# A causal attention and expert kernel: values one chunk later and split, maxima, projections and output products at other chunks

## The reference

```
l2 = max(norm(xn), 1e-12);  normed = xn / l2 * sqrt(128) * gamma
q, k, v = split(normed @ w_qkv)            # 16 heads of 64
sim = (q / 8) @ k^T, causal;  attn = softmax(sim)
attention = concat_heads(attn @ v) @ w_out
router_w = the two best of 8 experts, softmax of their logits
experts = layer_norm(xn + sum_e router_w[e] * (relu(xn @ W1[e]^T + b1[e]) @ W2[e]^T + b2[e]))
```

## Time and profile before

| | |
|---|---|
| median of 3 runs | 1487.04 us (1483.02 to 1488.01) |
| the profiled execution | 1485.95 us |
| its span | 1484.2 us |
| TensorE busy | 94% |
| VectorE busy | 74% |
| ScalarE busy | 71% |
| POOL busy | 64% |

### The profile page before, as it was taken

How to read it: one execution, slowest core, us unless ns; L and a number is a source line. 1 busy time by engine, 2 the same in 40 slices (tenths; PEclk the granted TensorE clock), 3 DMA queues, 4 the chain that set the end, 5 groups by cost and what they waited for, 6 DMA issues and landing times.

```text
span 1484.2 us, 27052 instructions
## 1 busy us (share of the span) xinstructions
PE 1396.8 (94%) x8618; PEld 1069.1 (72%) x8618; DVE 1104.8 (74%) x1928; ACT 1058.7 (71%) x2589; POOL 947.7 (64%) x933
## 2 busy tenths in 40 slices
PE   3689999599999999999999999999999999999996
PEld 3679999367777777777777777777777777777774
DVE  6645555458876987698769876987688768876985
ACT  2556666377777777777777777777777777777774
POOL 1774000168667866786678667866786678667775
PEclk9689999799999999999999999999999999999998
DMA  9122221122212221221122212221212121212112
GB/s 328 63 89 64 68 58 51 39 49 53 49 44 59 53 51 43 59 55 47 44 62 53 50 41 63 51 49 43 63 51 49 44 62 50 49 44 62 50 44 75
DMA packets 77226, 89.89 MB, mean 61 GB/s; under 512 B 17656, under 2 KB 54816, under 8 KB 77088
## 3 DMA queue, kind: packets, MB, share of 16 engines
q1 hardware_dynamic: 59168, 69.90, 18.6%
q10 hardware_dynamic: 13824, 9.86, 2.1%
q0 software_dynamic: 4096, 8.40, 2.0%
HBM read 37.25 MB, written 16.78 MB: 36 GB/s over the span
## 4 chain that ended last, share of the span: by engine, by line
PE 58%; DVE 11%; POOL 6%; issue 4%; ACT 2%; DMA 1%; SPq 0%; POOLq 0%
PE max_ps L1271 9%; PE head_ps L1313 7%; PE head_ps L1315 7%; PE head_ps L1317 7%; PE score_ps L1297 7%; PE score_ps L1296 6%; DVE row_max L1123 4%; POOL p_lo L1037 4%; PE misc_ps L1247 3%; PE misc_ps L1327 3%; POOL two_y L1030 2%; PE max_ps L1274 2%; PE misc_ps L1241 2%; PE score_ps L1299 2%; PE misc_ps L1243 2%
## 5 line engine op out<-in xcount | busy, mean ns | idle before, releaser
L1037 POOL TENSOR_TENSOR p_lo<-probs,p_hi 128x512 fp32r<-128x512 f32 (+3 forms) x768 | 805.5, 1068 | 322.5 <-ACT p_hi L1075 317.5
L1075 ACT ACTIVATE probs<-score_ps 128x512 f32<-128x512 f32 (+3 forms) x768 | 376.5, 490 | 211.8 <-PE score_ps L1299 116.7
L1123 DVE TENSOR_REDUCE row_max<-max_ps 128x1 f32<-128x128 f32 (+7 forms) x512 | 385.9, 754 | 174.0 <-PE max_ps L1274 169.0
L1075 ACT ACTIVATE p_hi<-score_ps 128x512 fp32r<-128x512 f32 (+3 forms) x768 | 375.3, 489 | 0.0
L1313 PE MATMUL head_ps<-p_hi,v_hi 128*65 128x512 f32 (+3 forms) x768 | 289.3, 377 | 2.2 <-POOL p_lo L1037 1.3
L1271 PE MATMUL max_ps<-k_a,q_a 128*128 128x384 f32 (+5 forms) x768 | 259.8, 393 | 26.2 <-DVE row_max L1123 20.8
L1296 PE MATMUL score_ps<-q_a,k_a 128*128 128x512 f32 (+3 forms) x768 | 266.5, 347 | 2.5 <-DMA q_b<-shift 2.5
L1297 PE MATMUL score_ps<-q_b,k_b 65*128 65x512 f32 (+3 forms) x768 | 267.7, 349 | 0.0
L1317 PE MATMUL head_ps<-p_lo,v_hi 128*65 128x512 f32 (+3 forms) x768 | 258.8, 337 | 0.0
L1315 PE MATMUL head_ps<-p_hi,v_lo 128*64 128x512 f32 (+3 forms) x768 | 258.7, 337 | 0.0
L1296 PEld LDWEIGHTS score_ps<-q_a,k_a 128*128 128x128 f32 x768 | 144.9, 189 | 45.2 <-issue 3.4
(11 more groups left out here) (162 smaller groups left out, 2193.6 us busy)
## 6 DMA issues: line engine op xcount, KB each, us to landing
k_a<-k_a SPq DMA_DIRECT2D x64, 256.0 KB, 4.0
q_b<-q_a SPq DMA_DIRECT2D x64, 256.0 KB, 4.8
scale<-inv_rows SPq DMA_DIRECT2D x128, 128.0 KB, 2.9
sorted_x<-zeros SPq DMA_DIRECT2D x13, 384.0 KB, 16.4
sorted_y<-result ACTq DMA_DIRECT2D x78, 64.0 KB, 1.7
w_raw<-sorted_x SPq DMA_DIRECT2D x25, 192.0 KB, 2.5
acc<-in_L_attn_x_dram SPq DMA_DIRECT2D x4, 512.0 KB, 6.9
w_raw<-in_L_ffn_W_dram ACTq DMA_DIRECT2D x1, 2048.0 KB, 23.2
```

What stands on the lines that cost most here:

```text
L1037: pool.tensor_tensor(p_lo[:, slot, 0:w], probs[:, n_chunk(g, c) % PROBS, 0:w], p_hi[:, slot, 0:w].bitcast(F32), ALU.subtract).then_inc(p_s ...
L1075: ins = act.activation(p[:, n_chunk(g, c) % ring, 0:width], score_ps[n_chunk(g, c) % 2][:, 0:width], ACT.Exp, scale=SCALE)
L1123: dve.tensor_reduce(row_max[:, g % 2, t:t + 1], src, axes, ALU.max).then_inc(max_taken, 1)
```

## The change

The values run five chunks behind their scores (LAG 5), and every step of the chain is due one chunk later. The values are split: `pv` makes the two products with p_hi, waits only for ScalarE, and stands right behind the score; `pv_low` makes the product with p_lo, waits for POOL, and stands behind the maximum. ScalarE's raw copy follows `pv_low`. Part 6 of the maxima moves from chunk 10 to 9, the last projection from chunk 10 to 8, the first y from chunk 11 to 10 and the second from chunk 10 to 8 of the odd head. One combine step of each head moves from chunk 4 to 7. In the experts' part the second register load is dropped.

```diff
--- before.py
+++ after.py
@@ -695,8 +695,7 @@
                             e_in = tile_experts[k]
                         if has(j, i, -2):
 
-                            inside = i is not None
-                            e_out = tile_experts[k - 2] if inside else expert_of(pe, j - 2)
+                            e_out = tile_experts[j - 2]
                         if k == 0 and i is None:
                             turn_rows(0, 0, None)
                         if has(j, i, 1):
@@ -814,15 +813,15 @@
             CH = len(chunks)
             DIAG = [q0 == j * P for _, j, q0 in chunks]
             WIDTH = [(half + 1) * BANK - q0 for half, _, q0 in chunks]
-            LAG = 4
-            CHAIN = [("fold", 5), ("invert", 8), ("store", 9), ("spread", 12), ("normalise", 16)]
+            LAG = 5
+            CHAIN = [("fold", 6), ("invert", 9), ("store", 10), ("spread", 13), ("normalise", 17)]
             CONSTS = 6
             G = BATCH * 2
             ALL_HEADS = PAIRS * G
             ALL_PAIRS = PAIRS * BATCH
 
             max_parts = [(0, 0), (1, 1), (2, 0), (3, 1), (7, None), (6, None), (5, None), (4, None)]
-            MAX_AT = [0, 1, 2, 3, 5, 7, 10, 11]
+            MAX_AT = [0, 1, 2, 3, 5, 7, 9, 11]
             FIRST_WIDE = {0: (4, 5), 1: (6,), 2: (7,)}
             FIRST_MAX_AT = [3, 4, 5, 6, 7, 8, 9, 10]
             PARTS = len(max_parts)
@@ -830,7 +829,7 @@
             HALF_MAX = [3, PARTS - 1]
             assert CH % 2 == 0
 
-            PROJECT_AT = [{1: 0, 2: 1, 3: 2, 5: 3, 6: 4, 10: 5}, {}]
+            PROJECT_AT = [{1: 0, 2: 1, 3: 2, 5: 3, 6: 4, 8: 5}, {}]
 
             GATHER_AT = [(1, c) for c in (6, 7, 8, 9, 10, 11)] + [(2, c) for c in (1, 3, 5)]
             COMBINE = ([("centre", q) for q in range(GROUP)] + [("first", q) for q in range(GROUP)]
@@ -838,8 +837,8 @@
                        + [("moments", 0), ("variance", 0)] + [("rsqrt", n) for n in range(RSQRT_STEPS)]
                        + [("scale", q) for q in range(GROUP)] + [("gamma", 0), ("beta", 0), ("sum", 0)])
             COMBINE_STEPS = len(COMBINE)
-            COMBINE_AT = [(g, c) for g in (3, 4, 5, 6, 7) for c in (0, 1, 4, 6, 8, 9, 10, 11)][:COMBINE_STEPS]
-            Y_AT = {11: 0, 22: 1}
+            COMBINE_AT = [(g, c) for g in (3, 4, 5, 6, 7) for c in (0, 1, 6, 7, 8, 9, 10, 11)][:COMBINE_STEPS]
+            Y_AT = {10: 0, 20: 1}
 
 
 
@@ -859,9 +858,14 @@
                     order.append(("score", g, c))
                 if g == 0 and c in FIRST_WIDE:
                     order += [("max", 0, m) for m in FIRST_WIDE[c]]
+                values = at >= LAG and (at - LAG) // CH < ALL_HEADS
+                if values:
+                    order.append(("pv", (at - LAG) // CH, (at - LAG) % CH))
                 max_at = MAX_AT if g else FIRST_MAX_AT
                 if g + 1 < ALL_HEADS and c in max_at:
                     order.append(("max", g + 1, max_at.index(c)))
+                if values:
+                    order.append(("pv_low", (at - LAG) // CH, (at - LAG) % CH))
 
                 if c in PROJECT_AT[g % 2] and g // 2 + 1 < ALL_PAIRS:
                     order.append(("project", g // 2 + 1, PROJECT_AT[g % 2][c]))
@@ -883,8 +887,6 @@
                     order.append(("combine", COMBINE_AT.index((r, c)), hp))
                 if r == G - 3 and c == 10 and hp + 1 < PAIRS:
                     order.append(("weights", 0, hp + 1))
-                if at >= LAG and (at - LAG) // CH < ALL_HEADS:
-                    order.append(("pv", (at - LAG) // CH, (at - LAG) % CH))
                 return order
 
             def numbered(order):
@@ -1082,7 +1084,7 @@
                             w_hi(act, c)
                         elif kind == "shift":
                             shifts(g, c, u)
-                        elif kind == "pv" and c in LAST:
+                        elif kind == "pv_low" and c in LAST:
                             half = LAST.index(c)
                             cols = slice(half * BANK, (half + 1) * BANK)
                             act.wait_ge(pv_done, n_chunk(g, c) + 1 + RING)
@@ -1303,7 +1305,7 @@
                         half, j, q0 = chunks[c]
                         i, s = g // 2 % 2, g % 2
                         width = (half + 1) * BANK - q0
-                        pe.wait_ge(p_split, n_chunk(g, c) + 1)
+                        pe.wait_ge(probs_ready, n_chunk(g, c) + 1 + 2)
                         if j == 0 and g:
 
                             pe.wait_ge(raw_out, n_half(g, half) - 1)
@@ -1314,6 +1316,13 @@
                                   start=(j == 0), stop=False)
                         pe.matmul(head_ps[0:HEAD, cols], v_lo[i][:, j, s], p_hi[:, slot, 0:width],
                                   start=False, stop=False)
+
+                    def low_values(g, c):
+                        half, j, q0 = chunks[c]
+                        i, s = g // 2 % 2, g % 2
+                        width = (half + 1) * BANK - q0
+                        slot, cols = (g * CH + c) % RING, slice(q0, (half + 1) * BANK)
+                        pe.wait_ge(p_split, n_chunk(g, c) + 1)
                         pe.matmul(head_ps[0:HEAD + 1, cols], v_hi[i][:, j, s], p_lo[:, slot, 0:width],
                                   start=False, stop=c in LAST).then_inc(pv_done, 1)
 
@@ -1339,6 +1348,8 @@
                             shifts(g, c, u)
                         elif kind == "pv":
                             values(g, c)
+                        elif kind == "pv_low":
+                            low_values(g, c)
                         elif kind == "y":
                             project_out(g, c, u)
 
```

## The result

| | before | after |
|---|---|---|
| median | 1487.01 us (1483.02 to 1488.01) | 1630.09 us (1625.45 to 1636.15) |
| span of the profiled execution | 1484.2 us | 1629.0 us |
| mean granted clock of TensorE | 0.975 | 0.931 |

The ratio is 1.097, with an interval of 1.0929 to 1.1012: 143 us more. The prediction had the sign and the largest cause, the fold behind the copies. It had 1544 us and a range that ended at 1588: it took the stops and the lower clock too small, and a second cause, the row maxima behind the moved y, it had with the wrong sign.

A forecast was written before the change was run, and what follows sets the result against it. The prediction took TensorE's own stream as the bound, with a little VectorE in even heads. From 1485.95 us: -33 (product order) - 7 (maxima) + 81 (late fold) + 17 (clock) = +58, giving 1544 us, range 1490 to 1588.

The forecast's parts named there:

- Edit 1: Product order inside a chunk on TensorE: 652 more mask products ahead of narrow weights, 33 us less (25 to 38).
- Edits 2 and 4: Values five chunks behind with third product after the maxima; expert register load dropped on TensorE's sequencer: nothing counted for either.
- Edit 5: Chain one chunk later: in even heads the fold queues behind q/k copies, y waits 2.7 us, 81 us more.
- Edit 3: Part 6 of the maxima at chunk 9: 20.8 us old waits off, 14 us new: net 7 us less.
- The last V projection at chunk 8 and the y at chunk 8 of odd heads have banks read two units earlier: Remark on the moved projection and second y, judged by their banks; counted at nothing.
- part 7 still comes before the next head's part 0: Order of the maxima in odd heads with combine steps; waits of 0.5 to 1.3 us expected, 14 us in all.
- Edit 6: TensorE's clock falls after one in three new waits, 10 x 1.7: 17 us more, bounds 0 and 51.
- Rival A: Fold overtakes the q/k copies in the transfer queue, y waits 0.3 to 0.5 us: 1458 us, chance 0.19.
- VectorE is then held only by v_lo: If the fold overtakes, even heads' normalise ends 4.3 us into chunk 8; y waits 0.3 to 0.5, 12 us.
- Rival B: About the same: wait for y about 1.3 us, partly hidden by stretched chunks 5 to 8; 1482 to 1491, chance 0.04.
- Rival C: Forecast's own ends: 2.3 us waits, no clock fall, 1501; 3.0 us, fall after each, 1587; forecast with these 0.75.
- Rival D: TensorE's loads do not set the 0.05 us per mask product, only the chain's delay is left: 1577 us, chance 0.02.

The follow-up runs named there:

- e8_lag5: Kernel before with new order of products, values five chunks behind, chain except fold a chunk later, second register load dropped; other places old: 1465.0 us.
- e12: Kernel after with fold one chunk earlier, last V projection back at chunk 10, second y back at chunk 10 of the odd head: 1469.43 us.
- e6: Kernel after with fold one chunk earlier (before the q/k copies) and last V projection back at chunk 10: 1512.91 us.
- e1: Kernel after with only the fold one chunk earlier, so issued before the q/k copies: 1556.58 us.
- e4_order: Kernel before with only the order of products changed, lag four and all places as before: 1465.67 us.

## Why the prediction was right and wrong

**The ledger.** The runs lead from one kernel to the other: before 1487.0; order of products, lag and register 1465.0 (e8_lag5); part 6, combine step and first y 1469.4 (e12, +4); second y 1512.9 (e6, +43.5); V projection 1556.6 (e1, +43.7); fold 1630.1 (+73.5). The last three steps are single edits, the first two are not. The parts hide each other, so they hold in this order only: the fold alone, on the kernel before, cost 140 us.

**Edit 1** was right in direction and nearly in size: 30 us for the 33 in pairs that wait for nothing else, of which the run of the order alone kept 20. The even heads give more of it and the odd ones less than I had spread it (15.3 us instead of the 15.1 I had named).

**Edits 2 and 4** were right: nothing (1465.0 us in e8_lag5 against 1465.7 in e4_order).

**Edit 5, the fold,** was right in its place and nearly in its times. Its size was low: (71.7 + 32.1 - 5.6 at the end) / 30 = 3.3 us for the 2.7, that is 98 us for the 81. I had worked out 2.3 to 3.0; 20 heads stand at the upper end, 2.97, and the third head of every eight at 3.9, which I had not worked out by itself. The term at fault is the normalise beside POOL. I had it end between 6.3 and 7.0 us into chunk 8 by how long it takes, 0.62 to 1.77; it ends by when POOL is done, 7.1 in 20 heads and 8.0 in the third of every eight, once 9.1. The Trainium skill, page "SBUF — State Buffer" (SBUF is the on-chip memory in which `raw`, `scale` and the probabilities lie), section "SBUF: two separate sides", says that whichever of a VectorE operation with two SBUF inputs and a GpSimd one starts first holds the shared ports for its whole instruction, and the other blocks. The trace after agrees where one p_lo is in the way (1.23 us in the head shown). The e1 trace agrees in kind, but one wait for one p_lo of 1.3 us does not give 4.32: VectorE did not get its turn between POOL's instructions either.

**Edit 3, the maxima, and "The last V projection at chunk 8 and the y at chunk 8 of odd heads have banks read two units earlier"** hold the step that failed outright. I priced the second y and the V projection at nothing by TensorE's banks, and did not ask what they put ahead of whom on VectorE. For the y I had seen part of it in edit 3: waits of 0.5 to 1.3 us behind the third and fifth odd head counted, 14 us, and all 20.8 us of old waits off, 7 us less in sum. The claim there that "part 7 still comes before the next head's part 0" holds on TensorE, but part 7 is reduced 1.60 us after the next head has begun, and part 0 waits for it. In the kernel after that makes the 16 stops of 1.50 to 1.88 us, and the waits for maxima rise from 20.8 to 37.1 us over the whole run: 16 us more, where I had 7 less. With the fold in order the second y alone is worth 43.5 us (e6 against e12), waits and clock together. The V projection is worth 43.7 us there (e1 against e6). In the kernel after its price is not shown: the reciprocal stands 2.06 us for the late fold after `v_lo` is done, so the one hides behind the other.

**Edit 6, the clock,** was right in direction and three times too small: 48.5 us for the 17. I had taken one fall in three waits and it was 27 in thirty, with nine more behind the stops of the maxima, which I had not counted at all; my own upper bound was 51.

**The sum** thus becomes -30 + 98 + 48.5 + 16 = 132.5, and some 10 us of the 143 stay open. The range ended at 1588 because its upper end kept the maxima at 7 us less and the wait at 3.0.

**Rival A** (1458 us if the fold were not late) was refuted twice: the fold did not overtake, and with it out of the way the change is still 4.8% slower. I had let "VectorE is then held only by v_lo" stand at 0.3 to 0.5 us; it was 1.24 and 4.04. **Rival B** had a wait of 1.3 us, and none was under 2.97. **Rival C**'s upper end was the nearest to the result. **Rival D** is out by e4.

## What to carry to other kernels

When a step moves past others, list for every queue it uses, the vector engine as well as the transfer queue, what now stands ahead of whom; a place priced by the buffers alone was wrong by 44 us twice here. Do not read a late consumer as the fault: letting y come later moved the same wait to the row maxima, and issuing the small transfer ahead of the big ones removed the wait for it (y itself was on time only with the V projection back as well). And a stop of the matrix engine that repeats in every second unit is to be priced with its clock: here half as much again as the wait itself.

## What the hardware showed that I had not expected

A VectorE multiplication with two SBUF inputs, 0.62 us when alone and 1.77 in the earlier trace rows, took 4.30 to 4.33 us in eight heads of e1 in which POOL did five subtractions without a gap, and ended only after the last of them. In the kernel after, 28 of the thirty late ones ended 0.54 to 0.56 us after the POOL subtraction that was running, wherever in it they had begun.

The length of a stop does not decide by itself whether the clock falls. In the kernel after, three of the stops of 2.97 us are not followed by a fall. The kernel before stops for 1.56 us seven times in the attention and the clock stays at 1.00. e6 stops in its attention for 1.51 to 1.55 us nine times and for 1.86 to 1.88 seven times, and the clock falls to 0.50, 1.2 GHz, within 1.7 us after two of the first and five of the second, such as this one:

```profile
545.07 0.33 PE L1273 MATMUL max_ps<-k_a,q_a 128*128 128x128 f32 x1 [1.87 <-DVE row_max L1125]
...
545.80:549.20 3.40, 3.40 (x12) 2.31 (x11) 0.69 (x4) 0.94 (x4) 0.45 (x1) 0.50 0.11 40
```

What sets the seven apart from the nine others was not tried.
